# Cross attention: sums of weights over four key blocks instead of two

## The reference, cut to what matters

```
q = jnp.einsum('bsc,hcd->bhsd', xn, wq)
k = jnp.einsum('btc,hcd->bhtd', yn, wk)
v = jnp.einsum('btc,hcd->bhtd', yn, wv)
a = jax.nn.softmax(jnp.einsum('bhsd,bhtd->bhst', q, k) * D ** (-0.5), axis=-1)
o = jnp.einsum('bhst,bhtd->bhsd', a, v)
```

## Time and profile before

| | us |
|---|---|
| median of three runs | 4375.98 (4366.36 to 4387.35) |
| the profiled execution | 4370.08 |
| its span | 4368.8 |
| TensorE busy in the span | 3679.5 (84%) |
| VectorE busy | 2304.0 (53%) |
| ScalarE busy | 1610.7 (37%) |
| GpSimd busy | 966.6 (22%) |
| additions into a_pair (L929) | 487.9 in 384 instructions, from 2575.8 to 3602.6 |

### The profile page before, as it was taken

How to read it: one execution, slowest core, us unless ns; L and a number is a source line. 1 busy time by engine, 2 the same in 40 slices (tenths; PEclk the granted TensorE clock), 3 DMA queues, 4 the chain that set the end, 5 groups by cost and what they waited for, 6 DMA issues and landing times. The chain is left out here.

```text
span 4368.8 us, 58721 instructions
## 1 busy us (share of the span) xinstructions
PE 3679.5 (84%) x22060; PEld 2145.7 (49%) x22060; DVE 2304.0 (53%) x4163; ACT 1610.7 (37%) x2945; POOL 966.6 (22%) x1022
## 2 busy tenths in 40 slices
PE   6679999989997973778866488999999995699998
PEld 4433444344433842444546344555555544576767
DVE  6647567466671344544435457666676524433332
ACT  1025546446463220233332024545545451122222
POOL 1100000000000011233223214555545453100000
PEclk9858979789896985789988769999999997899999
DMA  1111212112111202343420153443333411121111
GB/s 35 34 43 46 55 38 51 44 39 64 36 44 67 99 6 61 56 70 57 66 59 23 39 71 48 60 63 50 60 58 57 58 18 62 55 68 58 59 62 58
DMA packets 144194, 229.41 MB, mean 53 GB/s; under 512 B 40868, under 2 KB 90792, under 8 KB 140840
## 3 DMA queue, kind: packets, MB, share of 16 engines
q1 hardware_dynamic: 143912, 225.65, 24.5%
HBM read 99.39 MB, written 8.91 MB: 25 GB/s over the span
## 5 line engine op out<-in xcount | busy, mean ns | idle before, releaser
L893 DVE TENSOR_REDUCE a_mp<-bank 128x1 f32<-128x384 f32 (+2 forms) x1280 | 704.0, 592 | 464.2 <-PE bank L751 456.3
L859 ACT ACTIVATE a_p<-bank 128x512 f32<-128x512 f32 (+1 forms) x1088 | 593.8, 596 | 688.6 <-PE bank L776 664.3
L893 DVE TENSOR_REDUCE mx_mp<-bank 128x2 f32<-128x768 f32 (+4 forms) x640 | 597.8, 956 | 272.5 <-PE bank L751 161.5
L859 ACT ACTIVATE mx_p<-bank 128x512 f32<-128x512 f32 (+3 forms) x1088 | 549.1, 557 | 504.0 <-PE bank L776 287.6
L929 POOL TENSOR_TENSOR a_pair<-a_p 128x512 f32<-128x512 f32 x384 | 487.9, 1304 | 515.4 <-ACT a_p L859 515.4
L751 PE MATMUL bank<-a_ks,a_qs 96*128 96x384 f32 (+2 forms) x1280 | 448.3, 421 | 81.6 <-issue 59.2
L776 PE MATMUL bank<-a_qs,a_ks 98*128 98x512 f32 (+1 forms) x1088 | 428.2, 460 | 39.6 <-DMA a_qs<-a_mt 24.5
L751 PEld LDWEIGHTS bank<-a_ks,a_qs 96*128 96x128 f32 x1280 | 256.0, 201 | 237.7 <-issue 137.7
L776 PE MATMUL bank<-mx_qs,mx_ks 50*128 50x512 f32 (+3 forms) x1088 | 351.9, 507 | 21.4 <-DMA mx_qs<-mx_mt 13.4
L200 POOL TENSOR_TENSOR rs<-ve,neghalf 128x4 f32<-128x4 f32 (+2 forms) x80 | 75.3, 941 | 1329.2 <-DVE ve L195 1328.9
L751 PE MATMUL bank<-mx_ks,mx_qs 48*128 48x384 f32 (+4 forms) x1280 | 323.6, 448 | 12.9 <-issue 7.4
(11 more groups left out here) (294 smaller groups left out, 5553.7 us busy)
## 6 DMA issues: line engine op xcount, KB each, us to landing
sf_raw<-in_h_w SPq DMA_DIRECT2D x64, 512.0 KB, 3.5
a_ks<-a_kh SPq DMA_DIRECT2D x96, 192.0 KB, 4.5
ex_w<-in_L_ffn_w SPq DMA_DIRECT2D x16, 1024.0 KB, 4.9
a_qs<-a_qh SPq DMA_DIRECT2D x64, 256.0 KB, 6.1
mx_ks<-mx_kh SPq DMA_DIRECT2D x192, 48.0 KB, 2.1
a_ks<-a_kl SPq DMA_DIRECT2D x48, 192.0 KB, 5.2
mx_qs<-mx_qh SPq DMA_DIRECT2D x128, 64.0 KB, 2.2
mx_rec<-mx_flat SPq DMA_DIRECT2D x128, 64.0 KB, 2.0
```

The source lines that it names most:

```text
L859: act.activation(probs[place % len(probs)][0:kp, q0:T], self.bank(part, n, kb, h)[0:kp, q0:T], ACT.Exp, scale=scale).then_inc(*self.frees( ...
L893: v.tensor_reduce(best[:, tiled * j:tiled * j + tiled, i, ci], bank[:, 0:w] if tiled == 1 else bank[:, :, 0:w], AX.X, ALU.max).then_inc(*s ...
```

## The change: groups of four blocks

The additions are now chained over four blocks. At block 1 of a group (kb % 4 == 1) the tiles of blocks 0 and 1 are added into a_pair; at blocks 2 and 3 the tile of that block is added to a_pair in place. "Weights" is issued once for each group, after block 3 of it. Blocks 0 to 11 form 3 groups; block 12 stays alone. The waits move with it: an exponential that overwrites a tile waits for the addition of the tile's own block (for the first block of a group, that of the next), and the addition in place waits for the one before it on the same head. The first layer's attentions and the self attention have no pairs and are as before.

```
--- before.py
+++ after.py
@@ -617,7 +617,8 @@
                 if job.summed and part == 0:
                     yield from sums
                 yield "weigh", n, kb, part
-                if job.pairs and kb | 1 < last and kb % 2:
+                grouped = job.pairs and kb < (last + 1) // 4 * 4
+                if grouped and kb % 4:
                     for h in (2 * part, 2 * part + 1):
                         yield "pair", n, kb, h
                 if part:
@@ -625,7 +626,7 @@
                         held["q"] -= 1
                     if kb == last or P * (kb + 1) in [k0 for k0, _ in job.cuts]:
                         held["k"] -= 1
-                    if job.summed and (kb % 2 or not (job.pairs and kb | 1 < last)):
+                    if job.summed and (kb % 4 == 3 or not grouped):
                         due[half + 3].append(("weights", n, kb))
                     if kb == last:
                         due[half + 4].append(("result", n))
@@ -664,7 +665,7 @@
         pairs, summed = jobs[0].pairs, jobs[0].summed
         causal, upper = (any(j.mask == kind for j in jobs) for kind in ("causal", "upper"))
         blocks = lambda n: -(-jobs[n].nk // P)
-        paired = lambda n, kb: pairs and kb | 1 < blocks(n) - 1
+        grouped = lambda n, kb: pairs and kb < blocks(n) // 4 * 4
         HT, base = HG // tiled, [P // tiled * r for r in range(tiled)]
         tall = 3 * D + 2 if tiled == 1 else P
         kst = [sb(f"ks{i}", [tall, HT, max(cut_room)], F32R) for i in range(k_slots)]
@@ -812,12 +813,12 @@
                     m.then_inc(*up("values_summed", n, kb))
             elif part == "weights":
                 kb, = at
-                kp, first = min(P, job.nk - P * kb), kb == (1 if pairs else 0)
+                kp, first = min(P, job.nk - P * kb), kb == (3 if pairs else 0)
                 if first:
                     self.take(d_banks, "den", n)
                     pe.wait_ge(*self.empty("den", n))
                 for h in range(HG):
-                    if paired(n, kb):
+                    if grouped(n, kb):
                         pe.wait_ge(*has("pair_made", n, kb, h))
                         src = sums[h][:, :]
                     else:
@@ -852,9 +853,9 @@
                     if place >= len(probs):
                         m, mb, mh = list(weighed)[place - len(probs)]
                         if h % 2 == 0:
-                            act.wait_ge(*has("weights_summed" if summed and not paired(m, mb) else "values_summed", m, mb))
-                        if paired(m, mb):
-                            act.wait_ge(*has("pair_made", m, mb | 1, mh))
+                            act.wait_ge(*has("weights_summed" if summed and not grouped(m, mb) else "values_summed", m, mb))
+                        if grouped(m, mb):
+                            act.wait_ge(*has("pair_made", m, mb if mb % 4 else mb + 1, mh))
                     act.wait_ge(*self.full(part, n, kb, h))
                     act.activation(probs[place % len(probs)][0:kp, q0:T], self.bank(part, n, kb, h)[0:kp, q0:T], ACT.Exp, scale=scale
                                    ).then_inc(*self.frees(part, n, kb, h))
@@ -919,13 +920,18 @@
             job = jobs[n]
             if part == "pair":
                 kb, h = at
-                if kb > 1:
-                    g.wait_ge(*has("weights_summed", n, kb - 2))
-                elif n:
-                    g.wait_ge(*has("weights_summed", n - 1, blocks(n - 1) - 2))
-                for b in (kb - 1, kb):
-                    g.wait_ge(*self.freed("weigh", n, b, h))
-                even, odd = (probs[weighed[n, b, h] % len(probs)] for b in (kb - 1, kb))
+
+                odd = probs[weighed[n, kb, h] % len(probs)]
+                g.wait_ge(*self.freed("weigh", n, kb, h))
+                if kb % 4 == 1:
+                    if kb > 1:
+                        g.wait_ge(*has("weights_summed", n, kb - 2))
+                    elif n:
+                        g.wait_ge(*has("weights_summed", n - 1, blocks(n - 1) - 2))
+                    even = probs[weighed[n, kb - 1, h] % len(probs)]
+                else:
+                    g.wait_ge(*has("pair_made", n, kb - 1, h))
+                    even = sums[h]
                 g.tensor_tensor(sums[h][:, :], even[:, :], odd[:, :], ALU.add).then_inc(*up("pair_made", n, kb, h))
             elif part == "quotient":
                 for event in job.y_after():
```

## The result

The kernel with the change takes 4460.0 us (median of four runs, 4439.1 to 4466.4), the kernel before 4375.5 beside it. The ratio is 1.020 with a 95% interval of 1.016 to 1.023. Forecast were 4393 us and a range up to 4420, so the loss is 84 us and not 17. The profiled execution is the fastest of the four: 4439.1 us with a span of 4437.8, 69 us over the profiled one of before.

The account below looks back on a forecast made before the run. TensorE was taken as the bound, with GpSimd's closed loop of additions as a second. Stretches +12.3, corrections +1.2, +5.2, -1.5 and -0.6 gave +16.6 us; on the 4376.0 us median, 4393 us, range 4362 to 4420.

Parts of the forecast that it names:

- From the start of the first burst to the end of the third are 3 x 5.1 = 15.3 us: GpSimd's additions for a group of four blocks: three bursts of 5.1 us; with 2.85 us after them, at least 18.15 us.
- Costed at nothing: Exponentials' waits for additions (21.6 us in 29 waits) and an in-place addition's wait for the one before: no gain or loss.
- side by side with VectorE: Sign that the forecast is wrong: GpSimd's additions get slower than 1.3 us while VectorE works.
- if the bursts still have gaps while TensorE waits: Sign that the forecast is wrong: GpSimd's bursts of additions still have gaps while TensorE waits.
- The removal: Three "weights" steps fewer in each job, 48 in all at 0.86 us: 41 us, if TensorE's time is all that counts.
- the bounds: Least stretch lengths from GpSimd's additions: 18.15 us per group, 19.4 with the quotient, 20.95 with the residual, 23.1 for five blocks.
- about 50 was forecast: TensorE's loads at "weights" for a_pair (L825): their wait was to grow from 3.8 us to about 50.
- The last job: It has no maxima to take beside it; forecast to last 6 us longer.
- The sum over stretches: 48 stretches between bursts, each the greater of old length less 0.86 us and its bound: +12.3 us in total.
- the stretches even out: Rival: side work's order evens out stretches of the jobs, -14 us, 4362 us, no change; chance 0.13.
- The clock rival: Rival: TensorE's clock falls in new waits at "weights" in 18 stretches, about 22 us more, 4415 us; chance 0.16.

Follow-up runs that it names:

- the fifth: The changed kernel with maxima turned unsplit and split while read from the PSUM bank, and norms done by ScalarE: 4363.1 us, ratio 0.999.
- sixth: The kernel before with the same two moves as the fifth (maxima split from the PSUM bank, norms on ScalarE): 4372.8 us, ratio 1.001.
- both pairs: The fifth against the sixth; the seventh against the kernel before with the fifth's moves and its "weights" half a block later (4366.0 us, ratio 1.000).
- the seventh: The fifth with a group's "weights" half a block later and the next group's first two additions behind it: 4353.9 us, ratio 0.996; repeated, 4355.9 us.
- eleventh: The changed kernel with each addition waiting for the end of the one before it: 4436.4 us, ratio 1.014.
- the twelfth: The changed kernel with every second addition waiting for the end of the one before it: 4403.1 us, ratio 1.007.
- the first experiment: The changed kernel with VectorE's small copy of the row maxima replaced by a second maximum over the partial maxima: 4442.9 us, ratio 1.017.

## Why the prediction was wrong

- **The step that failed** is the one that made bursts of twelve additions a matter of GpSimd alone: "From the start of the first burst to the end of the third are 3 x 5.1 = 15.3 us", followed by the list of what now falls inside the bursts, which holds GpSimd's other work and nothing of VectorE's. An unbroken burst can hold VectorE's copies, norms and two-tile subtractions to its end. Taking them out brings back 90 us (97 by the medians), the falls of the clock behind them included: 47 to 54 for the maxima's split, 36 to 43 for the norms. "Costed at nothing" doesn't even name VectorE. The one sign of being wrong that does looks the other way, at additions that get slower "side by side with VectorE"; their median is 1.28 to 1.31 us, as before.
- **The trace of before had it.** The longest norms of before, shown above, took 2369 and 2572 ns where the median is 335 and 404. A maximum six or seven times the median asks which other engine was busy just then. Each of these lay under two of GpSimd's additions. For the additions the forecast read such a line; for VectorE it read none.
- **A test that it named came true**: it is wrong "if the bursts still have gaps while TensorE waits". They have, 2.62 us behind the held copy.
- **The removal and the bounds were right.** The bounds of 18.15, 19.4, 20.95 and 23.1 us are met within 0.5 us. Where nothing is held, the loads wait 44.6 us at "weights"; about 50 was forecast. The 384 multiplications are there, though busy for 74.0 us in the stage and not for 57. The last job lasts 6.4 us longer, as forecast, but it has a clock of 0.81 (below), and in the fifth, at 0.97, it is only 4.6: that agreement is in part luck.
- **The sum over stretches was biased even without the port.** Its rule (each stretch takes the greater of its old length less 0.86 and its bound) gives a loss of 12 us. Measured are -10 us (fifth against sixth) and a stage shorter by 12 us in jobs 1 to 14, which is the rival "the stretches even out" (-14). Side work moves from a stretch at its bound into one with room, so a stretch isn't a unit with a length of its own. (That is my reading; no run isolates it.) Of the 41 us of removed work some 30 are still lost in both pairs, and only part of that has a name: the 50 us of waits at "weights" in the fifth; the seventh has 11 of them and is 7 to 9 us faster than the fifth. The rest I leave open.
- **The clock rival was right that the clock would fall, and had the wrong place and too low a price.** It put 22 us on falls at "weights". There the fifth has 50 us of short waits and keeps its 0.98; two thirds of the time at the lower clock in after goes with the waits for held copies and norms. What the falls cost, no run isolates. As an estimate: TensorE's busy time in the stage is 988.8 us in after and 966.4 in the fifth, of which a_pair's multiplications have 74.0 and 96.2, so all its other work, which is the same but for the turning of the maxima, takes 45 us longer at 0.91 than at 0.98. That makes up about half of the 90 us. The last job of after does show 0.81 over its last 53 us, where the forecast, from 0.92 in the earlier trace rows, expected no more than one fall; so some of it did come at "weights":

```profile
3623.00:3676.00 53.00, 45.89 (x268) 15.74 (x264) 0.25 (x1) 25.55 (x46) 44.58 (x36) 0.81 0.03 6
```

The Trainium skill, in "SBUF — State Buffer" under "Who interferes with whom", says that copy, cast and tensor_scalar of VectorE, and its two-input operations when both inputs are in SBUF and GpSimd reads SBUF too, can take a port pair that GpSimd also needs, that it is locked for a whole instruction, and that the other engine stands until then. The runs agree on which instructions wait (copy, subtraction of two SBUF tiles, tensor_scalar) and which never do (the reductions). They differ on how long: by the rule, as an estimate, the eight held copies would have stood for one addition each at most, 8 x 1.28 = 10 us; they stood for 54, each over up to six additions.

## What to carry to other kernels

Before work is moved to GpSimd, list VectorE's SBUF-to-SBUF instructions in the same stretch and ask who waits for each: a long unbroken run of GpSimd additions can hold a 0.2 us copy to its end, and if TensorE waits for that copy, the run ends only when everything else stands. Then either take the operand from PSUM, give the instruction to ScalarE, or put a wait between the additions. And take the longest duration of a line as seriously as its median: that is where another engine's hold shows first.

## What I hadn't expected of the hardware

- **The hold outlasts an instruction, and a gap ends it.** With additions that overlap by some 0.03 to 0.07 us the copy took up to 7.22 us, to the end of the sixth. With gaps of 0.17 us it took 1.05 us at most, with gaps after every second addition 1.08. Norms went from 7.4 to 1.4 us (a_xb, eleventh).
- **Not every unbroken burst holds, and a gap isn't the only way in.** In after, six of the other copies came through at the end of an addition (0.41 to 1.03 us) and the subtraction behind each of them at the end of the next (1.2 us). The additions there overlap by 0.03 to 0.06 us, as they do where the copy was held. In the twelfth too four copies ended with the first of two additions that overlap. No run shows what decides it. In after the held copies all began under a block's first addition and the six others under its second, but in the first experiment subtractions that began under a second addition met both fates.
- **A wait can shorten a kernel**: a semaphore that orders nothing, 288 times, -57 us.
